# Masking the exponentials on GpSimd and VectorE instead of preloading transposed scores on TensorE, in an eight-stage attention chain

## The chip, the cores and the metric

The kernel runs on one core of a Trainium2 chip. The metric is device time in microseconds (us), the median of several runs. The trace is one further execution, recorded by the hardware profiler; its span runs from the first to the last instruction.

## The reference

The input is x, 16 sequences of 128 tokens by 256 features, in float32, with a context of the same shape. Four layers are applied one after another; together they are eight stages, named A0, A1, F0, A2, A3, A4, A5 and F1 in the kernel:

- A0: self-attention under a causal mask and a key mask. A1: attention over the context under the key mask. F0: feed-forward 256-1024-256 with Relu. Each is followed by adding the input and a layer norm with the unbiased standard deviation.
- A2: attention over the context, where mask[b, q, k] == 0 puts the score to -1e10. Norm.
- A3: attention over the context, scores multiplied by a weight per head and pair, and a mask per head and pair. Norm.
- A4: norm, attention over the context with no mask. A5: norm, self-attention under one mask of (query, key) that all sequences share. F1: norm, feed-forward with Gelu.

Every attention has 16 heads of 16 features: `softmax(mask(q k^T / 4)) v`, then an output product. A2 to A5 have biases on queries, keys, values and outputs. All arithmetic is float32.

## The kernel before

The 16 sequences are independent chains through the eight stages. Buffers exist for six of them at a time (SETS = 6), so that six are under way together. Each engine has one in-order list of steps, written out as strings of hexadecimal digits: a digit says which sequence does its next step on this engine (TENSOR, VECTOR, SCALAR, POOL, SYNC), and the steps of one sequence are those that `tensor_lane`, `vector_lane`, `scalar_lane`, `pool_lane` and `sync_lane` yield. PLACES gives each TensorE result one of eight PSUM banks. Semaphores alone tie the engines together.

One attention stage of one sequence goes so. TensorE transposes the input (xT, line 653), ScalarE copies it out (x_t, line 866), TensorE makes keys and queries with features on the partitions (K and Q, line 667). VectorE copies the keys twice, once multiplied by a 0/1 column for even heads and once for odd ones (k_eo, lines 986 and 990), and copies the queries, adding a bias (q_t, lines 999 and 1002). TensorE makes the scores with queries on the partitions (S, line 709), only to find each row's maximum: VectorE adds the mask and takes the maximum (L1018, one instruction and one read of its accumulator per head; L1023 where nothing is added). The maximum is split into two bf16 parts (high_low), transposed (mT) and copied (m_t, line 872). TensorE makes the scores again with keys on the partitions (ST, line 738), and adds minus the maximum to them by a small product (shift, line 749). In A0, A2 and A5 the four banks of ST are first filled with the mask, by one bf16 product of 128x512 each: `mask_bias(x, s)` against the identity (line 733). ScalarE takes the exponentials of four groups of four heads (exp, line 884, or 881 with a bias column in A1). TensorE multiplies by the values and a column of ones (PV, line 761), ScalarE copies the result (o_raw, line 889), TensorE transposes it (oT), VectorE divides (o_norm, lines 1044 and 1046), TensorE transposes again (nT), ScalarE copies (o_t, line 893), and TensorE makes the output product (O, line 660).

Then VectorE adds the residual (sum, line 1064), takes mean and variance (stats: `bn_stats` L1071, `bn_aggr` L1073, and a scale and epsilon L1075), GpSimd takes the root by a power (line 611), VectorE normalises (x_hat, line 1100), and GpSimd prepares the next residual (res, lines 621 to 629). In a feed-forward stage ScalarE makes the hidden units (h_t, line 903) in the buffers of exponentials, of which there are three.

Sync loads x, three masks and the context of each sequence (lines 513 to 523), the weights of each stage (line 530), and stores the result. In the first sequences the order is x of sequence 0, then x of sequence n with the three masks of sequence n - 1. The order lists begin with the transposes of five sequences on TensorE, and `bias` of all six on VectorE.

Of the kernel before, what the change touches and what calls it, by code (L numbers as in the profile page):

```python
# [17 lines left out]
KC = D // 128  # L18
# [3 lines left out]
EXP_BUFFERS, OUT_BUFFERS = 3, 2  # L22
# [34 lines left out]
PRELOADED = {"S": ("A1",), "ST": ("A0", "A2", "A5")}  # L57
CAPPED = [s for s in ("A0", "A2", "A5") if s not in PRELOADED["ST"]]
ADDED = [s for s in ("A0", "A2", "A5") if s not in PRELOADED["S"]]

# [17 lines left out]
POST_NORM = ("LN0", "LN1", "LN2", "LN3")  # L78

# [51 lines left out]
def vector_lane(x):  # L131
    yield "bias", "in"
    for s in STAGES:
        if x == 0:
            yield from (("folded", t) for t in FOLD_IN[s])
        if s in ATTN:
            if ATTN[s]["kv"] == "self":
                yield "k_eo", s
            yield "q_t", s
# [8 lines left out]
            if ATTN[s]["feeds"]:  # L148
                yield "k_eo", ATTN[s]["feeds"]
            if ATTN[s]["feeds"] and ATTN[ATTN[s]["feeds"]]["b"]:  # L150
                yield "v", ATTN[s]["feeds"]
            yield "o_norm", s
# [6 lines left out]
def scalar_lane(x):  # L159
    for s in STAGES:  # L160
        yield "x_t", s
        if s in FFN:
            yield from (("h_t", s, 0), ("h_t", s, 1))
            continue
        if ATTN[s]["kv"] == "self" and not ATTN[s]["b"]:
            yield "v", s
        yield "m_t", s
        yield from (("exp", s, j) for j in range(GROUPS))
        feeds = ATTN[s]["feeds"]
        yield "o_raw", s  # L170
        if feeds and not ATTN[feeds]["b"]:
            yield "v", feeds
        yield "o_t", s


def pool_lane(x):
    for s in STAGES:
        for n in LNS_AFTER[s]:
# [7 lines left out]
def sync_lane(x):  # L186
    yield from (("load_x", "in"), ("load_masks", "in"), ("load_ctx", "in"), ("load_weight", "in"), ("store", "out"))
# [4 lines left out]
21354113100100200244315050001000000110112020011310103012120222220100100020130022301233011121113133301100100012324040  # L192
21311042121020002000022221200130230021233040444411113111414103144121222230302002000200033333013001523454303022222204
22234123025300330000410231011004111155505540113441455443144455025050433334133332501004500001450441115411115155142551
20555015331135223112222225034031450504442061266146641144411431624662666662466415226124622332242631361633333432556623
13156625176666577366773422454457657657747757555744422656637752227672222333263333724743732356456747772776775375335727
24626742856768878873386666888733888838878485646333355768355548734684444554734586468885887478884834335877834439577776
99587997888999989999799789459864746956695855665644465459664875865498856499959898988945956754464594a798878aa77958a577
777a5a7a9aa9aaaa55556aa9a9a9576675a6859a9a96666867a67aaa5aa758575776aa5b7777bbabba7869996bbbb6bbbb6bb6ab9a99998b88a7
6969a9aabab76b66688688886a798a67a96987bbbbbb76bba6678686caacc7accaaaa8aabbcaccc8bacccc88cc887c7bca8877779ab8cbcbbb87  # L200
c7879b9b9978c999ccc7a88777d8dd8ccc9ccacaaac8998d88a8aaa88baac89dd9dddbdddcdddc9b9dcdbb9bbbbdbb8c8999bc9999b98ad9c88c
dc88e9eebabeedc9ccc9e9beeeeceececc9ceea9caeebbcbbcbbbba9ebe99ea999b9aa9cebaa9ceee9eeaaeecddaee9ab9addddddd9b9bdeccdc
aec9faffaefafadefdfffadccccdffffadffaefaaaabfedebbbdfbbbdfabecbeacbafdcbdddcffffddddfffeddafffdadfeefeedbaafdbfbfbba
deeeeeecffcebbbefbbcfbbebefdbdddbddddddffdbffdeffffcbbffbdfbdfdeeeefdedfdeeeddfddededdcececcccdcddfffddecfffffeffcef
ddfdcedddedecdeefeedfecfcedecffffffffeccefefdceefdffccccffecdceecfdffeeeeffceffcfecfcfcdfeffffeeeee
"""
VECTOR = """
01325411310100110000102234455001220202000012300003013121330111110102300012221100110021440422322424000001110220012330
03100212110132413333130104001010010000002220222002233200010530050434354325002200410151121211211111313340444410000501
13433133150124143105050005043241242222252221111505551252244415111500533011233311111514522534444406226624266664623134  # L210
33323363222246243343313166164236666636434444445452424353244645331735577565777223576746656722522223337533777266647437
77727323565424574346676536575455653555555557747286888888833333388774444848678653876688688548737547474768338484557585
85444394468995676699997946666666966888977559798559569888889996965794855664546469659577777777776777595558854a5aa79988
aaaa7a897a666a66aa9a5979755a797aaa9a7a6589799a97777788888888868685b868bbabbbb7ba6b6b6666a6a9ab6b89b9aab7a7bbb7b8b869
9a97aa6968a78a6ab88877777876cccacccc8caab888b8caaacbbccb9ca98999c99999999b7bccbc7878c78cb9caa88aaaaaaaa7daadda88888c
# [976 lines left out]
```

## Time and profile before

| | |
|---|---|
| Median of 3 runs | 1177.99 us (1177.74 to 1178.14) |
| The profiled execution's own time | 1174.8 us |
| Its span | 1173.0 us |
| TensorE matmuls busy | 1135.5 us, 97% |
| TensorE weight loads busy | 934.6 us, 80% |
| VectorE busy | 853.0 us, 73% |
| ScalarE busy | 475.9 us, 41% |
| GpSimd busy | 206.3 us, 18% |
| Mean granted TensorE clock | 0.994 of full speed |

Busy time is the time in which at least one instruction of the engine runs; instructions on one engine overlap a little, so the mean of one times its count can be more. Of the time outside TensorE's matmuls, 37.5 us, most lies in the first 30 us.

### The profile page before, as it was taken

The numbers are of one execution on the slowest core, as the hardware profiler recorded it, in microseconds if no ns is written. First come the engines' busy times: TensorE is split into PE (matmuls) and PEld (weight loads), VectorE is DVE, ScalarE is ACT, GpSimd is POOL, SyncE is SP. The second block draws the span as 40 slices with busy tenths as digits, with TensorE's granted clock in tenths as the row PEclk, the third lists the DMA queues.
The fourth block names the chain that finished last, engine by engine and source line by source line (L and its number), as shares of the span: only waits on it lengthen the run. The fifth ranks groups of instructions, "written<-read, shape, count | busy, mean of one in ns | idle before, by whom it ended". The sixth has DMA issues, their size and how long they took to land.

```text
span 1173.0 us, 36188 instructions
## 1 busy us (share of the span) xinstructions
PE 1135.5 (97%) x14100; PEld 934.6 (80%) x14100; DVE 853.0 (73%) x3467; ACT 475.9 (41%) x1118; POOL 206.3 (18%) x319
## 2 busy tenths in 40 slices
PE   4999999999999999999999999999999999999998
PEld 3878788878888888787887888887878887887678
DVE  4667679596789586777878767787697848687861
ACT  1243343334443434334444434434435344444353
POOL 0012212121111030212102021211111212211110
PEclk9999999899999999999999999999999999999999
DMA  6700010101010100101010010011001100011000
GB/s 245 321 2 2 2 47 2 46 2 47 18 58 11 42 14 6 47 19 47 14 52 13 6 47 18 2 63 47 14 6 52 58 3 2 6 51 47 2 3 18
DMA packets 22950, 44.05 MB, mean 38 GB/s; under 512 B 6528, under 2 KB 16896, under 8 KB 19712
## 3 DMA queue, kind: packets, MB, share of 16 engines
q1 hardware_dynamic: 21824, 40.30, 9.8%
q8 instruction: 116, 1.90, 0.7%
q10 hardware_dynamic: 960, 1.44, 0.3%
q14 instruction: 50, 0.41, 0.1%
HBM read 39.63 MB, written 2.10 MB: 36 GB/s over the span
## 4 chain that ended last, share of the span: by engine, by line
PE 82%; DVE 12%; issue 3%; SPq 1%; DMA 1%; ACT 0%; POOL 0%; DVEq 0%; POOLq 0%; ACTq 0%
PE bank L667 22%; PE bank L660 21%; PE bank L761 8%; PE bank L738 7%; PE bank L709 7%; PE bank L653 7%; PE bank L733 4%; DVE bank L1018 3%; PE bank L723 2%; PE bank L749 2%; DVE neg_max L1018 2%; DVE neg_max L1023 1%; PE bank L774 1%; PE bank L813 1%; DVE x_sum L1064 1%
## 5 line engine op out<-in xcount | busy, mean ns | idle before, releaser
L884 ACT ACTIVATE exps_t<-bank 128x512 f32<-128x512 f32 x320 | 169.4, 608 | 92.2 <-PE bank L749 91.9
L611 POOL TENSOR_TENSOR root<-var_eps,halves 128x1 f32<-128x1 f32 x128 | 74.0, 578 | 729.6 <-DVE var_eps L1075 729.2
L1018 DVE CUSTOM_DVE_ANT_0 bank<-bank,bias 128x128 f32<-128x128 f32 x512 | 130.0, 324 | 14.5 <-PE bank L709 14.1
L667 PE MATMUL bank<-x_t,weights_A 128*128 128x128 f32 x1024 | 134.9, 280 | 1.1 <-ACT x_t L866 1.0
L667 PEld LDWEIGHTS bank<-x_t,weights_A 128*128 128x128 f32 x1024 | 124.9, 193 | 9.1 <-issue 2.1
L667 PE MATMUL bank<-x_t,weights_F 128*128 128x128 f32 x1024 | 124.4, 277 | 0.8 <-ACT x_t L866 0.6
L667 PEld LDWEIGHTS bank<-x_t,weights_F 128*128 128x128 f32 x1024 | 118.8, 192 | 3.9 <-ACT x_t L866 1.3
L660 PE MATMUL bank<-weights_F,exps_t 128*128 128x256 f32 x512 | 120.4, 381 | 0.2 <-DVE x_t L1046 0.2
L709 PE MATMUL bank<-k_eo,q_t 32*128 32x256 f32 x1536 | 109.3, 398 | 3.0 <-DVE q_t L1002 2.2
L761 PE MATMUL bank<-exps_t,v_one 128*32 128x128 f32 x3072 | 108.5, 279 | 2.8 <-ACT exps_t L884 2.3
L903 ACT ACTIVATE exps_t<-bank,weights_F 128x128 f32<-128x128 f32 x256 | 73.0, 368 | 84.1 <-PE bank L667 83.7
L1018 DVE DVE_READ_ACCUMULATOR2_ANT neg_max<- 128x1 f32 x768 | 106.3, 138 | 0.0
L660 PEld LDWEIGHTS bank<-weights_F,exps_t 128*128 128x128 f32 x512 | 93.7, 190 | 12.5 <-DVE x_t L1046 0.4
L660 PE MATMUL bank<-weights_A,q_t 128*128 128x256 f32 x384 | 101.2, 389 | 2.2 <-ACT q_t L893 2.0
L738 PEld LDWEIGHTS bank<-q_t,k_eo 32*128 32x128 f32 x2560 | 80.4, 187 | 26.7 <-issue 25.3
L866 ACT COPY x_t<-bank 128x256 f32<-128x256 f32 x128 | 47.7, 378 | 132.6 <-PE bank L653 131.8
L761 PEld LDWEIGHTS bank<-exps_t,v_one 128*32 128x32 f32 x3072 | 77.7, 110 | 26.8 <-ACT exps_t L884 11.5
L889 ACT COPY o_raw<-bank 128x512 f32<-128x512 f32 x96 | 55.1, 587 | 107.7 <-PE bank L761 105.2
L738 PE MATMUL bank<-q_t,k_eo 32*128 32x128 f32 x2560 | 95.7, 284 | 0.6 <-issue 0.6
L1023 DVE TENSOR_REDUCE neg_max<-bank 128x4 f32<-128x512 f32 x128 | 81.1, 681 | 17.2 <-PE bank L709 17.0
L709 PEld LDWEIGHTS bank<-k_eo,q_t 32*128 32x128 f32 x1536 | 72.0, 185 | 19.9 <-issue 12.3
L986 DVE SCALAR_TENSOR_TENSOR k_eo<-bank,parity,k_bias_A 128x256 f32<-128x256 f32 x128 | 55.9, 478 | 35.2 <-PE bank L667 21.9
(103 smaller groups left out, 1820.0 us busy)
## 6 DMA issues: line engine op xcount, KB each, us to landing
weight<-in_fside SPq DMA_DIRECT2D x16, 1024.0 KB, 4.9
weights_A<-in_weights_A SPq DMA_DIRECT2D x4, 1028.0 KB, 18.1
weights_F<-in_weights_F SPq DMA_DIRECT2D x2, 2054.0 KB, 16.4
drop_raw<-in_drop SPq DMA_DIRECT2D x16, 256.0 KB, 5.3
x_hat<-in_x SPq DMA_DIRECT2D x16, 128.0 KB, 3.1
out<-x_sum SPq DMA_DIRECT2D x16, 128.0 KB, 1.7
ctx_t<-in_ctx_t SPq DMA_DIRECT2D x13, 128.0 KB, 3.7
rows_A<-in_rows_A SPq DMA_DIRECT2D x3, 512.0 KB, 19.8
```

Of the source, the lines that this page charges most:

```text
L611: nc.gpsimd.tensor_tensor(root[x][:], var_eps[x][:], halves[:, e:e + 1], ALU.pow).then_inc(done["root"], 1)
L653: mm = nc.tensor.matmul(dst[:, 128 * c:128 * c + 128], src[:, 128 * c:128 * c + 128], id32[:], start=True, stop=True, is_transpose=True)
L660: mm = nc.tensor.matmul(dst, left[:, c, :], right[:, c, :], start=(c == 0), stop=(c == total - 1))
L667: mm = nc.tensor.matmul(dst[:, 128 * f:128 * f + 128], w[:, c, 128 * f:128 * f + 128], tokens_t[:, c, :], start=(c == 0), stop=(c == KC - 1))
L709: mm = nc.tensor.matmul(score_bank(x, "S", s, j)[:, 256 * c:256 * c + 256], q_t[x][group_rows(j), c, :], k_eo[x][group_rows(j), c, :, :], ...
L738: mm = nc.tensor.matmul(score_bank(x, "ST", s, j)[:, 128 * n:128 * n + 128], k_eo[x][group_rows(j), n // 2, n % 2, :], q_t[x][group_rows(j ...
L761: mm = nc.tensor.matmul(bank((x, "PV", s, 0))[32 * n:32 * n + 32, 128 * j:128 * j + 128], v_one[x][:, VE * head(j, n):VE * head(j, n) + 2 ...
L884: nc.scalar.activation(dst, score_bank(x, "ST", s, j)[:], ACT.Exp, scale=DH ** -0.5).then_inc(done["exp"], 1)
L903: ins = nc.scalar.activation(hidden(x, s)[:, f, :], src[:, 128 * n:128 * n + 128], ACT.Gelu if FFN[s]["gelu"] else ACT.Relu, bias=b_1[s][: ...
L986: ins = nc.vector.scalar_tensor_tensor(out=k_eo[x][:, :, odd, :], in0=src, scalar=parity[:, odd:odd + 1], in1=k_bias[s][:, odd, :].unsquee ...
L1018: ins = nc.vector.tensor_tensor_reduce(out=heads[:, n, :], in0=heads[:, n, :], in1=mask_bias(x, s), scale=-1.0, scalar=2.0 ** 126, op0=ALU ...
L1023: nc.vector.tensor_reduce(neg_max[x][:, j, :], heads, AX_X, ALU.max, negate=True).then_inc(done["max"], 1)
```

## The change

- The mask products of line 733 are gone from A0, A2 and A5. The exponentials are taken unmasked and then lowered. In A0 ScalarE adds the key mask as a bias column, and GpSimd sets the pairs of a later key to zero with `affine_select`. In A2 and A5 VectorE takes the minimum with a bf16 tile of 2^-100 or 2 (0 or 2 in A5), made from transposed masks. TensorE's PV waits for that step instead of for exp.
- ScalarE takes over the query copy with its bias (two Identity instructions where there is one) and the even and odd key copies of A0 and A1, which have no bias.
- The variance: the residual sum also accumulates its row sum, a small instruction makes minus the mean, and ScalarE squares the centred row with an accumulator, into x_hat as scratch. `bn_stats` and `bn_aggr` remain for LN5 alone.
- Key masks of all sequences are loaded by two DMAs behind x of sequence 0. The pair mask comes in two versions (plain and transposed), in three buffers, the first three behind the weights of F0. The A0 weights come in two halves.
- All order strings and bank places are new. TensorE has the same 1607 steps; its order now starts with the transposes of sequences 1 to 5 and then K, Q of 1. It ends with one sequence alone: behind the last Y of sequence e stand PV, oT, nT, O, xT, H and Y of f. Before, the last 33 us held steps of c, d, e and f.

```diff
-PRELOADED = {"S": ("A1",), "ST": ("A0", "A2", "A5")}
+LEAST = 2.0 ** -100
+PRELOADED = {"S": ("A1",), "ST": ()}
...
+SQUARED = [n for n in LN if n != "LN5"]
+SUMMED = [s for s in STAGES if LNS_AFTER[s]]
...
+        def load_keys(queue):
+            queue.dma_start(key_rows[:].rearrange("p b n -> p (b n)"), dram["kmask"].rearrange("b c d e -> (c d) (b e)")
+                            .broadcast_to([128, B * N])).then_inc(keys_loaded, 16)
+            queue.dma_start(key_cols[:], dram["kmask_t"]).then_inc(keys_loaded, 16)
+        def load_pairs(queue, x):
+            at = x % PAIR_BUFFERS
+            queue.dma_start(ik_raw[at][:], whole("ik", x)).then_inc(pairs_loaded[at], 16)
+            queue.dma_start(ik_t_raw[at][:], whole("ik_t", x)).then_inc(pairs_loaded[at], 16)
...
                 load_x(sp, 0)
+                load_keys(sp)
                 for x in range(1, SETS):
                     load_x(sp, x)
-                    load_masks(sp, x - 1)
-                load_masks(sp, SETS - 1)
...
+                def hide_later(x, s, j):
+                    pool.wait_ge(done["exp"], nth(x, "exp", s, j))
+                    e = exps_t[EXP_AT[x, s]][:, slots(j), :]
+                    nc.gpsimd.affine_select(out=e, in_=e, compare_op=ALU.is_ge, fill=0.0, base=0,
+                                            pattern=[[0, GH], [1, N]], channel_multiplier=-1).then_inc(done["later"], 1)
...
-                    if masked:
-                        if s == "A5":
-                            pe.wait_ge(sxs_made, 1)
-                        else:
-                            pe.wait_ge(done["bias"], nth(x, "bias", "in"))
-                        for j in range(GROUPS):
-                            nc.tensor.matmul(free_bank((x, "ST", s), j)[:], mask_bias(x, s), four(idb[:]), start=True, stop=True)
...
-                    pe.wait_ge(done["exp"], nth(x, "exp", s, j))
+                    made = "later" if s == "A0" else "keep" if s in ("A2", "A5") else "exp"
+                    pe.wait_ge(done[made], nth(x, made, s, j))
...
+                    elif kind == "k_eo":
+                        src = free_keys(act, x, s)
+                        act.wait_ge(parity_made, 4)
+                        for odd in range(2):
+                            ins = nc.scalar.activation(k_eo[x][:, :, odd, :], src, ACT.Identity, scale=parity[:, odd:odd + 1])
...
+                            for c in range(KC):
+                                ins = nc.scalar.activation(q_t[x][:, c, :], src[:, c, :], ACT.Identity,
+                                                           bias=q_bias[s][:, c:c + 1])
...
+                    elif kind == "square":
+                        act.wait_ge(means_made, norm_turn(VECTOR_ORDER, "sum", x, LN[s]["after"][1], SUMMED))
+                        nc.scalar.activation(x_hat[x][:], x_sum[x][:], ACT.Square, bias=neg_mean[x][:, 0:1],
+                                             accum_out=squares[x][:]).then_inc(done["square"], 1)
...
+                    nc.vector.tensor_scalar(pair_most[x][:], ik_t_raw[at][:], 0.0, 2.0, ALU.not_equal, ALU.mult
+                                            ).then_inc(pairs_kept, 1)
+                    dve.wait_ge(pairs_kept, 2 * nth(x, "pairs", "in"))
+                    nc.vector.tensor_scalar(pair_most[x][:], pair_most[x][:], LEAST, None, ALU.max).then_inc(done["pairs"], 1)
...
+                def keep_seen(x, s, j):
+                    dve.wait_ge(done["exp"], nth(x, "exp", s, j))
...
+                    nc.vector.tensor_tensor(e, e, four(most), ALU.min).then_inc(done["keep"], 1)
...
+                    if s in SUMMED:
+                        nc.vector.tensor_tensor_reduce(out=x_sum[x][:], in0=src[:, 0:D], in1=residual[:], scale=1.0, scalar=0.0,
+                                                       op0=ALU.add, op1=ALU.add, accum_out=row_sum[x][:]).then_inc(done["sum"], 1)
+                        dve.wait_ge(done["sum"], nth(x, "sum", s))
+                        nc.vector.tensor_scalar(neg_mean[x][:], row_sum[x][:], -1.0 / D, None, ALU.mult).then_inc(means_made, 1)
...
+                    if n in SQUARED:
+                        dve.wait_ge(done["square"], nth(x, "square", n))
+                        nc.vector.tensor_scalar(var_eps[x][:], squares[x][:], 1.0 / (D - d["ddof"]),
+                                                0.0 if d["on_root"] else d["eps"], ALU.mult, ALU.add).then_inc(done["stats"], 1)
+                        return
```

## Rows read from the trace of the kernel before

**Rows 1.** The page's first part: busy time and share of the span by engine.
```profile
PE 1135.5 (97%) x14100; PEld 934.6 (80%) x14100; DVE 853.0 (73%) x3467; ACT 475.9 (41%) x1118; POOL 206.3 (18%) x319
```
**Rows 2.** Chain that ended last, by engine.
```profile
PE 82%; DVE 12%; issue 3%; SPq 1%; DMA 1%; ACT 0%; POOL 0%; DVEq 0%; POOLq 0%; ACTq 0%
```
**Rows 3.** Busy time by stretch; columns: length, PE, PEld, DVE, ACT, POOL, clock, DMA.
```profile
0.00:10.00 10.00, 0.00 (x0) 0.00 (x0) 1.82 (x23) 1.28 (x1) 1.54 (x12) 1.00 0.61 193
10.00:20.00 10.00, 6.29 (x30) 5.12 (x31) 2.51 (x16) 1.86 (x5) 0.00 (x0) 1.00 0.47 148
20.00:30.00 10.00, 7.82 (x78) 6.74 (x77) 8.74 (x48) 0.75 (x2) 0.00 (x0) 1.00 1.03 409
...
1140.00:1173.00 33.00, 29.74 (x262) 26.25 (x250) 6.17 (x18) 12.91 (x36) 2.55 (x4) 1.00 0.05 17
```
**Rows 4.** Line 733 among the groups by line on PE.
```profile
L733 PE MATMUL bank<-idb,bias 128*128 128x512 bf16 x128 | 34.6, 388 | 1.3 <-DVE v_one L1121 0.4 <-DVE k_eo L990 0.4 <-DVE neg_max L1018 0.2
...
L733 PE MATMUL bank<-idb,sxs_bias 128*128 128x512 bf16 x64 | 16.7, 380 | 0.0
```
**Rows 5.** Pieces of the chain that ended last: start, length, what.
```profile
1138.08 0.86 PE bank L733 x4
```
**Rows 6.** The start in order of time: start, length, engine, line.
```profile
10.73 1.09 PE L653 MATMUL bank<-id,x_hat 128*128 128x128 f32 x4 [10.73 <-DMA x_hat<-in_x]
...
16.60 4.08 PE L667 MATMUL bank<-x_t,weights_A 128*128 128x128 f32 x24 [0.46 <-ACT x_t L866]
...
22.87 1.15 PE L709 MATMUL bank<-k_eo,q_t 32*128 32x256 f32 x16 [2.18 <-DVE q_t L1002]
```
**Rows 7.** Groups by line on DVE.
```profile
L1018 DVE DVE_READ_ACCUMULATOR2_ANT neg_max<- 128x1 f32 x768 | 106.3, 138 | 0.0
L1071 DVE BATCH_NORM_STATS2 bn<-x_sum 128x6 f32<-128x256 f32 x128 | 54.0, 422 | 2.0
L1133 DVE SCALAR_TENSOR_TENSOR weight<-drop_raw,weight 128x512 f32<-128x512 uint8 x64 | 44.6, 697 | 0.9
...
L1064 DVE TENSOR_TENSOR x_sum<-bank,x_hat 128x256 f32<-128x256 f32 x80 | 33.5, 420 | 58.7 <-PE bank L660 58.4
L999 DVE TENSOR_TENSOR q_t<-bank,q_bias_A 128x256 f32<-128x256 f32 x80 | 33.4, 419 | 28.9 <-PE bank L667 28.7
L990 DVE TENSOR_SCALAR k_eo<-bank,parity 128x256 f32<-128x256 f32 x64 | 27.9, 477 | 21.5 <-PE bank L667 11.8 <-issue 9.7
...
L1073 DVE BATCH_NORM_AGGREGATE mean_var<-bn 128x2 f32<-128x6 f32 x128 | 23.3, 182 | 4.4
...
L1075 DVE TENSOR_SCALAR var_eps<-mean_var 128x1 f32<-128x1 f32 x128 | 19.7, 154 | 4.4
```
**Rows 8.** Groups by line on ACT.
```profile
L884 ACT ACTIVATE exps_t<-bank 128x512 f32<-128x512 f32 x320 | 169.4, 608 | 92.2 <-PE bank L749 91.9
L903 ACT ACTIVATE exps_t<-bank,weights_F 128x128 f32<-128x128 f32 x256 | 73.0, 368 | 84.1 <-PE bank L667 83.7
...
L866 ACT COPY x_t<-bank 128x256 f32<-128x256 f32 x128 | 47.7, 378 | 132.6 <-PE bank L653 131.8
L881 ACT ACTIVATE exps_t<-bank,col_bias 128x512 f32<-128x512 f32 x64 | 39.3, 688 | 22.0 <-PE bank L749 21.8
...
L903 ACT ACT_TABLE_LOAD x15 | 19.2, 1283 | 0.3
```
**Rows 9.** Groups by line on POOL.
```profile
L611 POOL TENSOR_TENSOR root<-var_eps,halves 128x1 f32<-128x1 f32 x128 | 74.0, 578 | 729.6 <-DVE var_eps L1075 729.2 <-PE bank L653 0.2
L621 POOL TENSOR_TENSOR x_hat<-x_hat,rows_A 128x256 f32<-128x256 f32 x48 | 35.0, 730 | 103.0 <-PE bank L653 102.0 <-DVE x_hat L1100 0.9
...
L590 POOL TENSOR_SCALAR_AFFINE_SELECT id<-id 128x128 f32<-128x128 f32 x1 | 0.3, 292 | 0.2 <-POOL causal L585 0.2
```
**Rows 10.** DVE and POOL instructions in order of time, around 754 us.
```profile
754.06 1.08 DVE L1133 SCALAR_TENSOR_TENSOR weight<-drop_raw,weight 128x512 f32<-128x512 uint8 x1
...
754.68 1.05 POOL L626 TENSOR_TENSOR x_hat<-x_hat,rows_F 128x256 f32<-128x256 f32 x1
```

More of the change, by code:

```diff
@@ L54 @@
 STAGES = ["A0", "A1", "F0", "A2", "A3", "A4", "A5", "F1"]
[L57 to L59 removed]
+LEAST = 2.0 ** -100
+PRELOADED = {"S": ("A1",), "ST": ()}
+ADDED = ("A0", "A2", "A5")
 LN = {
@@ L147, in vector_lane @@
             yield "high_low", s
-            if ATTN[s]["feeds"]:
+            if ATTN[s]["feeds"] and ATTN[ATTN[s]["feeds"]]["b"]:
                 yield "k_eo", ATTN[s]["feeds"]
+            if s in ("A2", "A5"):
+                yield from (("keep", s, j) for j in range(GROUPS))
             if ATTN[s]["feeds"] and ATTN[ATTN[s]["feeds"]]["b"]:
@@ L163, in scalar_lane @@
             yield from (("h_t", s, 0), ("h_t", s, 1))
+            yield from (("square", n) for n in LNS_AFTER[s] if n in SQUARED)
             continue
+        if ATTN[s]["kv"] == "self" and not ATTN[s]["b"]:
+            yield "k_eo", s
+        yield "q_t", s
         if ATTN[s]["kv"] == "self" and not ATTN[s]["b"]:
@@ L169, in scalar_lane @@
         feeds = ATTN[s]["feeds"]
+        if feeds and not ATTN[feeds]["b"]:
+            yield "k_eo", feeds
         yield "o_raw", s
@@ L173, in scalar_lane @@
         yield "o_t", s
+        yield from (("square", n) for n in LNS_AFTER[s] if n in SQUARED)
 def pool_lane(x):
     for s in STAGES:
+        if s == "A0":
+            yield from (("later", s, j) for j in range(GROUPS))
         for n in LNS_AFTER[s]:
@@ L422, in program @@
         ctx_loaded = sems("ctx_loaded")
-        masks_loaded = sems("masks_loaded")
+        keys_loaded = sem("keys_loaded")
+        first_loaded = sem("first_loaded")
+        pairs_loaded = [sem(f"pairs_loaded{x}") for x in range(PAIR_BUFFERS)]
         stored = sems("stored")
@@ L426, in program @@
                                               "H", "Y", "fold")}
-        done |= {k: sem(f"done_{k}") for k in ("x_t", "v_copy", "m_t", "exp", "o_raw", "o_t", "h_t")}
-        done |= {k: sem(f"done_{k}") for k in ("bias", "folded", "k_eo", "q_t", "v", "times", "lower", "max", "high_low", "o_norm", "sum",
+        done |= {k: sem(f"done_{k}") for k in ("x_t", "square", "v_copy", "k_copy", "q_t", "m_t", "exp", "o_raw", "o_t", "h_t")}
+        done |= {k: sem(f"done_{k}") for k in ("bias", "pairs", "folded", "k_eo", "v", "times", "lower", "max", "high_low", "keep", "o_norm", "sum",
                                                "stats", "x_hat")}
-        done |= {k: sem(f"done_{k}") for k in ("root", "res")}
+        done |= {k: sem(f"done_{k}") for k in ("root", "res", "later")}
         key_bias_made = sem("key_bias_made")
+        pairs_kept = sem("pairs_kept")
         high_made = sem("high_made")
         recip_made = sem("recip_made")
+        rows_summed = sem("rows_summed")
+        means_made = sem("means_made")
         bn_made = sem("bn_made")
@@ L551, in _ @@
                 load_stage(sp, "F0")
+                for x in range(PAIR_BUFFERS):
+                    load_pairs(sp, x)
                 load_stage(sp, "A2")
@@ L780, in shift_products, with weights_loaded @@
                     return mm
+                def weights_loaded(s, part):
+                    if s == "A0" and part == "first":
+                        pe.wait_ge(first_loaded, 16)
+                    else:
+                        pe.wait_ge(stage_loaded[s], all_loaded(s))
                 def norm_folded(s, part):
```

281 lines of the change are left out of this document (158 added, 123 removed).

## The prediction, made before the changed kernel was run

> **What bounds the kernel now.** I read the busy shares first: TensorE 97%, VectorE 73%, ScalarE 41%, GpSimd 18% [rows 1]. A busy TensorE need not be the bound, so the chain of waits comes next: followed back from the end, 82% of the span is TensorE work, 12% VectorE's [rows 2]. Both views say that TensorE's instruction stream is the limit nearly everywhere, and that in some stretches VectorE is late for it. So work taken off TensorE shortens the span at full price, unless what remains is held up elsewhere; work taken off or put on the others counts only through waits.
>
> Then the stretches. The span of 1173.0 less 1135.5 busy leaves 37.5 us in which no matmul runs. I split it with the view by stretch [rows 3]: 10.0 + 3.7 + 2.2 = 15.9 us in the first 30 us; 3.3 us in the last 33 us; so 18.3 us in the 1110 us between, 1.6% of them. These three parts are predicted separately.
>
> **The mask products.** There are 128 + 64 = 192 of them [rows 4]. Their own duration, 0.38 us, is latency and overlaps the next; on the chain four of them take 0.86 us [rows 5], 0.215 us each. 192 x 0.215 = 41.3 us go. The scores behind them stay as they are. Since TensorE is on the path, 41.3 us is the first term; bounds are 36 us (if the 12% of the chain that is VectorE's gives its share back as waiting) and 51 us (the two groups' busy time, 34.6 + 16.7 [rows 4], which counts overlap).
>
> **The start.** TensorE begins at 10.73 us, held by x, and the first keys at 16.60, because the order wants five transposes first and the last x is issued late, behind twelve mask DMAs; then it waits 2.18 us for queries which VectorE copies behind its mask work, itself late by those DMAs [rows 6]. After the change two larger DMAs stand in place of those twelve ahead of the last x, and the first queries and keys go through ScalarE, which does nothing then. The first ten microseconds carry 193 GB/s [rows 3]: 0.77 MB of x, 0.26 MB of keys and the 1 MB of weights at that rate are 10.5 us. So I put the first keys at 11 us and no wait of 2 us behind them: idle 11 in place of 15.9, a gain of 5 us. Bounds: 0 if the weights now arrive last, 8 if the DMAs move as fast as between 20 and 30 us (409 GB/s [rows 3]). The pair masks and their transposed copies, 32 of 64 KB, leave the start; later Sync queues them in its list as it did the old ones, with nothing urgent behind, so nothing.
>
> **The end.** Before, four sequences fill TensorE to within 3.3 us, most of it the last sum and store. In the new order sequence f is alone behind e's last product. Its chain there: exponentials 0.6 each and minima 0.7 each, begun behind the sum of e, 2.4 us beyond what TensorE does meanwhile; o_raw 0.6, reciprocal and division 0.7, o_t 0.4; sum, mean, square, scale, root and x_hat 0.5 + 0.2 + 0.5 + 0.2 + 0.6 + 0.4 = 2.4; x_t 0.4; a dozen hand-overs of 0.1, 1.2 (durations as in [rows 7 to 9]). That is 8.1 us, plus the same 2.6 for last sum and store: 10.7 against 3.3, a loss of 7.5 us. Bounds: 4 (if half of those waits are covered by e's last matmuls) and 12 (if e and f, two sequences where there were four, already leave gaps a stage earlier).
>
> **VectorE.** Off it go the query copies, 96 x 0.419 = 40.2; the plain key copies, 27.9; 112 of 128 `bn_stats`, 47.3, and `bn_aggr`, 20.4: 135.8 us [rows 7]. On it come 128 minima over 128x512 with two SBUF inputs. The nearest row is L1133, 0.697 [rows 7]: 89.2 us. Below, they could cost 0.42, the row for half the elements (53.8 us); above, 1.08, what L1133 took once (138 us). Further 112 small mean instructions like L1075, 17.2; 112 sums with an accumulator, dearer by one read of 0.138, 15.5, and at least nothing; the pair masks' two more small ones for 16 sequences, about 7. Together 129 us. Net -7: VectorE stays near 846 us, 75% of the shorter span. It is no more the bound than before, but TensorE leaves it 41 us less room.
>
> That 1.08 has a cause in the trace: L1133 at 754.06 overlaps a GpSimd addition at 754.68, and both are longer than usual (1.08 for 0.697, 1.05 for about 0.73) [rows 7, 9, 10]. The Trainium skill, GPSIMD Engine Reference, section Specifications, says the same: the SBUF interfaces are shared, with contention for VectorE instructions with two SBUF inputs. The new minima are such instructions. With GpSimd busy a fifth of the time and 0.35 us more where they meet, 128 x 0.22 x 0.35 = 10 us on VectorE, which wipes out its net saving and is in my range, not in the sum.
>
> **ScalarE.** 160 biased halves of queries at 0.368 and 16 copies at 0.378 are 65; 64 key copies at 0.378 + 0.080 (what a column operand adds, 0.688 - 0.608) are 29; 112 squares at 0.46 + 0.14 are 67 [rows 8]. 476 + 161 = 637 us, 56%. Hidden by TensorE, for which ScalarE waited most of the time (idle before its rows, all ended by PE [rows 8]). If the cover is gone, each query copy is late by 0.2 us: 80 x 0.2 = 16 us at worst.
>
> **GpSimd.** 64 selects over 128x512. At 128x128 one took 0.292 [rows 9]. Bounds are 0.3 (all fixed cost) and 1.35 (0.73 for 256 elements with two inputs, scaled with the overhead kept); I take 0.9: 58 us, 206 becomes 264 us, 23%. Behind a select that waits for its exponential stand roots of other sequences; behind those x_hat on VectorE. Five other sequences cover it.
>
> **Latency per sequence.** A0 gains 4 x 0.9, A2 and A5 4 x 0.7 less their overlap with exponentials, norms 0.3 more. Some 10 us on a chain which has six sequences' time, 1173 x 6 / 16 = 440 us, for itself. Nothing in the middle; its 18.3 us I leave at 18.3.
>
> **The sum.** 1173.0 - 41.3 - 5.0 + 7.5 = 1134.2 us of span. The profiled execution took 1.8 us more than its span: 1136.0. The median of runs is 3.2 us above the profiled one (1177.99 against 1174.8), so runs should give 1139 us.
>
> **Rivals.**
> 1. The gain is held back. VectorE and ScalarE become late in more stretches: with 41 us less TensorE work, a stretch in which VectorE ends last gains nothing. For it speaks the chain's 12%; against it, only 1.6% of the middle is idle. Price: 12% of 41 us, the 10 us of contention, and a few us of queries on ScalarE: 18 us, 1157 us.
> 2. The start gives 8 and the end takes only 2, since f's lone chain is partly covered, and the middle's idle time shrinks by 5, as its waits for m_parts, exponentials and queries are of 0.5 us each and in new places: 1178 - 41.3 - 8 + 2 - 5 = 1126 us.
> 3. Slower: table loads. A load takes 1.283 us [rows 8]. Today they come only where Gelu and Exp alternate in ScalarE's list (29 times, 31 in the new one); Copy and Relu need none. If Square isn't in Exp's table, each of 112 squares brings two loads, 2.57 us, 287 us on ScalarE: 924 us, above VectorE, and 2.6 us more in each norm, with exponentials queued behind. It outweighs the gain of 39 us once 0.35 us of each 2.57 surfaces on TensorE; at a sixth it does, 1186 us. The Trainium skill, ScalarE: Activation LUTs, section Table sets, says that cheap functions such as relu, copy and identity are in every set, and doesn't list square there. This trace agrees for relu and copy, and shows nothing of the other two.
> 4. The change doesn't do what it says: if the exponentials' extra hand-over delayed PV so that TensorE idles 0.4 us at each of 96 PV groups of A0, A2 and A5, the product's saving would be gone: 1178 us. Against it: PV of other sequences stand between in the order.
>
> **How the numbers follow.** The forecast 0.57, rival 1 0.19, rival 2 0.20, rival 3 0.02, rival 4 0.02. A change is told from none here at about 0.2%, 2.4 us. Faster: 0.57 + 0.19 + 0.20 = 0.96, to which half of rival 4 adds 0.01; same 0.01; slower 0.02. The likeliest case alone reaches from 1130 to 1148, by the bounds of the start, the end and the mask products. The range of eight in ten goes to rivals 1 and 2: 1125 to 1156 us.
>
> **What would show it.** TensorE busy near 1094 us and no line 733; first keys on TensorE near 11 us; the last 35 us with 10 us idle; VectorE's share at 75%, ScalarE's at 56%, minima near 0.7 us, selects near 0.9; table loads about 30 as now. The prediction is wrong if TensorE's idle time in the middle passes 30 us (rival 1), if table loads pass 200 (rival 3), or if matmuls left in place change their pitch.

## The result, and the profile after

The changed kernel takes 1159.94 us (median of 3 runs, 1159.59 to 1161.37); before it was 1177.99. The ratio is 0.9881 (95% interval 0.9853 to 0.9910): faster by 18 us, where 39 were forecast, and outside the range of 1125 to 1156. The profiled execution took 1159.94 us, its span is 1157.7. Two single executions, of 1415 us in experiment 5 and of 3640 us in experiment 10, stood far apart from the others of their kernels and are in none of the ratios below.

First the busy time by engine, from the page of the changed kernel; it answers to [rows 1].
```profile
PE 1106.9 (96%) x13908; PEld 921.1 (80%) x13908; DVE 841.3 (73%) x3468; ACT 618.6 (53%) x1584; POOL 258.8 (22%) x383
```
The 192 products are gone (14100 less 13908 matmuls). VectorE, ScalarE and GpSimd are where the prediction put them (846, 637 and 264). TensorE isn't: 1106.9 us busy where 1135.5 - 41.3 = 1094.2 were expected, and 1157.7 - 1106.9 = 50.8 us idle, where 18.3 + 11 + 10.7 = 40 were. So more than half of what is missing lies in TensorE's busy time, which is not all work at full pace.

Where that idle time lies is told by the view by stretch (columns as in [rows 3]), of the changed kernel:
```profile
0.00:30.00 30.00, 19.79 (x163) 16.79 (x164) 13.78 (x112) 9.39 (x23) 1.55 (x12) 1.00 0.95 343
30.00:100.00 70.00, 68.66 (x912) 56.59 (x910) 42.53 (x199) 36.70 (x94) 21.25 (x33) 0.98 0.25 100
100.00:1000.00 900.00, 881.40 (x11298) 738.27 (x11297) 686.53 (x2780) 498.83 (x1284) 212.66 (x304) 1.00 0.08 27
1000.00:1124.70 124.70, 114.08 (x1368) 91.18 (x1367) 89.92 (x341) 62.26 (x158) 22.07 (x33) 0.99 0.07 25
1124.70:1157.70 33.00, 22.98 (x177) 18.24 (x175) 8.54 (x41) 11.40 (x28) 1.27 (x2) 0.79 0.02 8
```
and of the kernel before, the two stretches that the rows ahead of the prediction don't have:
```profile
100.00:1000.00 900.00, 888.80 (x11184) 733.91 (x11183) 683.12 (x2752) 376.68 (x885) 171.45 (x258) 1.00 0.08 26
1000.00:1140.00 140.00, 134.19 (x1710) 106.52 (x1712) 108.02 (x419) 57.56 (x132) 23.51 (x34) 1.00 0.06 23
```
Length less the first busy number is TensorE's idle time. In the first 30 us it is 10.2 (15.9 before, 11 predicted). In the last 33 us it is 10.0 (3.3 before, 10.7 predicted). Between them it is 30.6 us (1.34 + 18.60 + 10.62), where it was 18.4 (1.36 + 11.20 + 5.81) and was left at 18.3. The last stretch has one number more: the granted clock is 0.79, where it was 1.00 before [rows 3].

The view of TensorE's waits, changed kernel (for what, us in total, times, longest):
```profile
PE bank L707 <- DMA x_hat<-in_x: 9.3, 1, 9.3
PE bank L707 <- DVE x_hat L1205: 6.9, 10, 2.7
PE bank L808 <- DVE exps_t L1083: 6.1, 18, 1.1
PE bank L721 <- ACT x_t L931: 3.8, 8, 0.6
```
and one row of the same view of the kernel before:
```profile
PE bank L653 <- DVE x_hat L1100: 1.4, 3, 0.5
```
The third row is a wait that the kernel before didn't have: L808 is PV, and L1083 the minimum in place. The second is the norm, 6.9 us for 1.4. What the new instructions cost, by the groups by line:
```profile
L1083 DVE TENSOR_TENSOR exps_t<-exps_t,pair_most 128x512 f32<-128x512 f32 x64 | 44.9, 750 | 0.0
L1083 DVE TENSOR_TENSOR exps_t<-exps_t,sxs_most 128x512 f32<-128x512 f32 x64 | 44.4, 739 | 9.8 <-ACT exps_t L971 9.7
...
L1158 DVE DVE_READ_ACCUMULATOR2_ANT row_sum<- 128x1 f32 x112 | 9.2, 82 | 0.0
L953 ACT ACTIVATE x_hat<-x_sum,neg_mean 128x256 f32<-128x256 f32 x112 | 57.2, 511 | 85.1 <-DVE neg_mean L1161 84.5
L953 ACT ACTIVATION_READ_ACCUMULATOR x_hat<-x_sum,neg_mean 128x1 f32 x112 | 21.3, 190 | 0.0
L990 ACT ACT_TABLE_LOAD x16 | 20.5, 1283 | 0.3
L971 ACT ACT_TABLE_LOAD x14 | 18.0, 1283 | 5.2 <-PE bank L714 5.0
...
L645 POOL TENSOR_SCALAR_AFFINE_SELECT exps_t<-exps_t 128x512 f32<-128x512 f32 x64 | 43.5, 709 | 100.6 <-ACT exps_t L968 100.5
```
Minima at 0.74 to 0.75 us, 89.3 us in all (0.697 and 89.2 predicted); selects 0.71 (0.9). Squares bring no table loads: there are 30 in these two groups and 32 in all.

The start, TensorE in order of time (start, length); it answers to [rows 6]: transposes at 9.33 us, keys at 12.73 where it was 16.60, and no wait for the queries ahead of L763.
```profile
9.33 2.94 PE L707 MATMUL bank<-id,x_hat 128*128 128x128 f32 x10 [9.33 <-DMA x_hat<-in_x]
12.73 5.17 PE L721 MATMUL bank<-x_t,weights_A 128*128 128x128 f32 x24 [0.46 <-ACT x_t L931]
17.83 1.15 PE L763 MATMUL bank<-k_eo,q_t 32*128 32x256 f32 x16
```

The end. First the last sequence alone, in order of time, then the same stretch cut into windows (the number behind POOL's is the granted clock):
```profile
1133.08 0.43 PE L808 MATMUL bank<-exps_t,v_one 128*32 128x128 f32 x8 [1.12 <-DVE exps_t L1083]
...
1138.90 2.05 PE L714 MATMUL bank<-weights_A,q_t 128*128 128x256 f32 x4 [0.55 <-ACT q_t L980]
1143.65 0.66 PE L707 MATMUL bank<-id,x_hat 128*128 128x128 f32 x2 [2.71 <-DVE x_hat L1205]
1144.86 6.57 PE L721 MATMUL bank<-x_t,weights_F 128*128 128x128 f32 x32 [0.55 <-ACT x_t L931]
1151.27 3.62 PE L714 MATMUL bank<-weights_F,exps_t 128*128 128x256 f32 x16
```
```profile
1124.70:1133.00 8.30, 7.26 (x85) 6.15 (x83) 4.45 (x31) 5.90 (x14) 0.00 (x0) 1.00 0.01 2
1133.00:1138.00 5.00, 2.65 (x38) 1.34 (x38) 2.50 (x6) 0.59 (x1) 0.00 (x0) 0.90 0.08 26
1138.00:1144.00 6.00, 2.74 (x8) 1.47 (x6) 1.16 (x5) 0.97 (x3) 0.97 (x2) 0.50 0.00 0
1144.00:1151.00 7.00, 6.45 (x32) 6.17 (x31) 0.00 (x0) 2.80 (x6) 0.30 (x1) 0.53 0.00 0
```
TensorE is busy half of the five microseconds from 1133 on, and the granted clock falls from 1.00 (2.4 GHz) through 0.90 to 0.50 (1.2 GHz). At that level the output projection takes 2.05 us, and the 32 matmuls of the last feed-forward's first half 6.57. In the kernel before, with TensorE full there, they took:
```profile
1154.20 1.03 PE L660 MATMUL bank<-weights_A,q_t 128*128 128x256 f32 x4
...
1163.03 3.81 PE L667 MATMUL bank<-x_t,weights_F 128*128 128x128 f32 x32 [0.55 <-ACT x_t L866]
```
1.0 + 2.8 us, with two pairs of short transposes (0.66 for the 0.41 that they take in experiment 4) 4.3 us. The last 33 us aren't all of it. A few us earlier, behind a wait of 1.12 us, 16 matmuls take 3.51 us, which in experiment 4 take 2.02; the stretch from 1110 to 1124.7 has a granted clock of 0.88. So the rows show 4.3 + 1.5 = 5.8 us.
```profile
1116.81 3.51 PE L721 MATMUL bank<-x_t,weights_A 128*128 128x128 f32 x16 [0.55 <-ACT x_t L931]
```
The Trainium skill, TensorE: Matmul & The Clock Gate, section Why this matters for your kernels, warns of idle gaps between bursts of matmuls, behind which the clock is back at half. The trace agrees that the clock falls where TensorE waits between bursts, but the page speaks of single gaps longer than any in this stretch: in the last stretch the clock is down after idle pieces of 1.12, 0.85 and 0.90 us, before the one wait of 2.71.

A wait in pieces also lengthens the busy time. The 32 matmuls of one PV step take 1.08 us in one piece, as in experiment 2 at this place. In the last sequence here each eight of them wait for their minimum and take 0.43 us, 1.72 together, besides the waits between.

### The profile page after: what moved, and what is told of

Same layout as the page of the kernel before. It is cut to its first block and busy times, and to the rows that moved or that the text cites. A ratio compares the mean times of both kernels' runs of the same rounds, so it can differ in the third digit from the quotient of the medians.

```text
span 1157.7 us, 36414 instructions
## 1 busy us (share of the span) xinstructions
PE 1106.9 (96%) x13908; PEld 921.1 (80%) x13908; DVE 841.3 (73%) x3468; ACT 618.6 (53%) x1584; POOL 258.8 (22%) x383
## 5 line engine op out<-in xcount | busy, mean ns | idle before, releaser
L663 POOL TENSOR_TENSOR root<-var_eps,halves 128x1 f32<-128x1 f32 x128 | 76.9, 602 | 609.9 <-DVE var_eps L1171 588.1
L971 ACT ACTIVATE exps_t<-bank 128x512 f32<-128x512 f32 x256 | 135.7, 605 | 34.3 <-PE bank L795 33.8
L721 PE MATMUL bank<-x_t,weights_A 128*128 128x128 f32 x1024 | 139.3, 284 | 2.7 <-ACT x_t L931 2.1
L721 PEld LDWEIGHTS bank<-x_t,weights_A 128*128 128x128 f32 x1024 | 127.3, 197 | 12.1 <-ACT x_t L931 4.5
L721 PE MATMUL bank<-x_t,weights_F 128*128 128x128 f32 x1024 | 127.9, 281 | 2.8 <-ACT x_t L931 1.7
L721 PEld LDWEIGHTS bank<-x_t,weights_F 128*128 128x128 f32 x1024 | 121.6, 195 | 9.1 <-ACT x_t L931 3.1
L808 PE MATMUL bank<-exps_t,v_one 128*32 128x128 f32 x3072 | 114.5, 277 | 8.2 <-DVE exps_t L1083 6.1
L763 PE MATMUL bank<-k_eo,q_t 32*128 32x256 f32 x1536 | 107.7, 396 | 2.6 <-issue 1.7
L808 PEld LDWEIGHTS bank<-exps_t,v_one 128*32 128x32 f32 x3072 | 74.5, 109 | 40.1 <-DVE exps_t L1083 15.1
L953 ACT ACTIVATE x_hat<-x_sum,neg_mean 128x256 f32<-128x256 f32 x112 | 57.2, 511 | 85.1 <-DVE neg_mean L1161 84.5
L784 PEld LDWEIGHTS bank<-q_t,k_eo 32*128 32x128 f32 x2560 | 82.1, 186 | 16.8 <-issue 12.7
L968 ACT ACTIVATE exps_t<-bank,col_bias 128x512 f32<-128x512 f32 x128 | 80.4, 695 | 27.9 <-PE bank L795 27.8
L1116 DVE TENSOR_REDUCE neg_max<-bank 128x4 f32<-128x512 f32 x128 | 81.4, 681 | 18.4 <-PE bank L763 18.4
L763 PEld LDWEIGHTS bank<-k_eo,q_t 32*128 32x128 f32 x1536 | 72.6, 185 | 20.0 <-issue 13.6
```

What stands on the lines that cost most here:

```text
L663: nc.gpsimd.tensor_tensor(root[x][:], var_eps[x][:], halves[:, e:e + 1], ALU.pow).then_inc(done["root"], 1)
L721: mm = nc.tensor.matmul(dst[:, 128 * f:128 * f + 128], w[:, c, 128 * f:128 * f + 128], tokens_t[:, c, :], start=(c == 0), stop=(c == KC - 1))
L763: mm = nc.tensor.matmul(score_bank(x, "S", s, j)[:, 256 * c:256 * c + 256], q_t[x][group_rows(j), c, :], k_eo[x][group_rows(j), c, :, :], ...
L784: mm = nc.tensor.matmul(score_bank(x, "ST", s, j)[:, 128 * n:128 * n + 128], k_eo[x][group_rows(j), n // 2, n % 2, :], q_t[x][group_rows(j ...
L808: mm = nc.tensor.matmul(bank((x, "PV", s, 0))[32 * n:32 * n + 32, 128 * j:128 * j + 128], v_one[x][:, VE * head(j, n):VE * head(j, n) + 2 ...
L953: nc.scalar.activation(x_hat[x][:], x_sum[x][:], ACT.Square, bias=neg_mean[x][:, 0:1], accum_out=squares[x][:]).then_inc(done["square"], 1)
```

## The experiments

Each was run beside the kernel before on its chip; ratios are to that kernel. A difference of 0.001 is 1.2 us. The intervals are 0.2 to 0.3% either way, so a difference between two of these ratios is uncertain by 3 to 5 us. The changed kernel's 0.9881 was taken apart from the ratios below, beside a kernel before at 1177.99 us where theirs is at 1173 to 1174; differences against it carry that too.

**1. The products alone taken away**, in the old orders. The masks of the transposed scores are left out; nothing stands for them.
```
-                        for j in range(GROUPS):
-                            nc.tensor.matmul(free_bank((x, "ST", s), j)[:], mask_bias(x, s), four(idb[:]), start=True, stop=True)
```


> The kernel before, with its own orders, and with the 192 mask products taken out and nothing put in their place (the exponentials of A0, A2 and A5 are left unmasked). Theory (the products were worth their full price, and the changed kernel gives part of it back in waits for the steps that it adds): 1178 - 41 = 1137 us, within 4. Rival (the products hid something, weight loads or late engines, so that their removal is worth half): 1150 to 1158 us whatever the orders.

0.9786 (0.9760 to 0.9811): 25.6 us below its kernel before (1148.57 against 1174.16). Page:
```profile
PE 1102.5 (96%) x13908; PEld 926.4 (81%) x13908; DVE 852.4 (74%) x3467; ACT 477.3 (42%) x1118; POOL 206.3 (18%) x319
```
TensorE's busy time falls by 33.0 us of the 41.3, and its idle time rises from 37.5 to 43.1. The products are not worth their full price; some 16 us are missing. Only 5.6 of them are idle time. The 8.3 that busy time falls short by stand mostly in the scores behind the products, which the prediction took to stay as they are (busy time, mean ns; first the kernel before, then this one):
```profile
L738 PE MATMUL bank<-q_t,k_eo 32*128 32x128 f32 x2560 | 95.7, 284 | 0.6 <-issue 0.6
L731 PE MATMUL bank<-q_t,k_eo 32*128 32x128 f32 x2560 | 104.6, 286 | 1.4 <-DVE k_eo L983 0.6 <-DVE v_one L1114 0.3
```
The group is busy 8.9 us longer without the products in front. What holds it up was not taken apart.

**2. The lowering taken away** from the changed kernel: no selects, no minima, PV waits for the exponential.
```
-                    made = "later" if s == "A0" else "keep" if s in ("A2", "A5") else "exp"
+                    made = "exp"
```


> The changed kernel with its 64 selects on GpSimd and 128 minima on VectorE left out, so that PV follows the exponentials at once (the exponentials are left partly unmasked). Theory (PV's waits for the lowering steps, and VectorE's 89 us in them, are the largest part of what came back): 10 to 16 us less than 1160, about 1147 us. Rival (the new orders are loose by themselves): under 4 us less, 1156 to 1160 us.

0.9755 (0.9737 to 0.9773), 0.0126 below the changed kernel: the lowering costs 15 us. The prediction had it in the lone chain at the end only, and at no time in the middle. Page, and two rows of the end:
```profile
PE 1098.9 (96%) x13908; PEld 921.0 (81%) x13908; DVE 755.5 (66%) x3340; ACT 617.6 (54%) x1584; POOL 208.8 (18%) x319
```
```profile
1121.26 1.08 PE L808 MATMUL bank<-exps_t,v_one 128*32 128x128 f32 x32
...
1130.45 5.35 PE L721 MATMUL bank<-x_t,weights_F 128*128 128x128 f32 x32 [0.55 <-ACT x_t L931]
```
Half of the 15.6 us of span are idle time (43.2 for 50.8) and half TensorE's busy time (8.0 us). Of the latter, 4.2 are PV's (its group is busy 110.3 us for 114.5), and 2.7 are the clock's, which falls later at the end of this kernel: the output projection takes 1.10 us for 2.05, the transposes 0.41 for 0.66 twice, the last feed-forward's first half 5.35 for 6.57.

**3. The variance back on VectorE**, in the new orders: `bn_stats`, `bn_aggr` and a plain sum; squares skipped.
```
-SQUARED = [n for n in LN if n != "LN5"]
+SQUARED = []
```


> The changed kernel with the variance as before: bn_stats and bn_aggr on VectorE for all eight norms, a plain residual sum, no squares on ScalarE. Orders unchanged. Theory (the norm's way over ScalarE and back is late for the next transpose): TensorE's waits for x_hat fall from 6.9 us towards the 1.4 of before, about 1155 us. Rival (VectorE is what is short, and bn_stats costs it 35 us net): 1160 to 1168 us.

1.0109 (1.0082 to 1.0137): 27 us slower than the changed kernel, and far outside what either side expected. Page and waits:
```profile
PE 1121.5 (94%) x13908; PEld 928.2 (78%) x13908; DVE 886.6 (75%) x3468; ACT 561.6 (47%) x1360; POOL 258.8 (22%) x383
```
```profile
PE bank L708 <- DVE x_hat L1207: 15.2, 23, 2.5
```
45 us more on an engine that is 73% busy cost 27 us. Its busy share says little; the waits for the norm double (15.2 for 6.9 us). Half of the 29.3 us of span is TensorE's busy time again (14.6), at a mean granted clock of 0.984 for 0.990.

**4. Dummy products near the end** of the changed kernel: 40 of 128x512 with constant operands (the text below says 39; the numbers of the edit add up to 40, and 13948 matmuls ran for 13908), in two banks that nothing reads by then, placed among the last 35 steps of TensorE's order. They add no result.
```
+                filler = {-35: 1, -30: 1, -26: 2, -25: 4, -24: 2, -21: 2, -12: 5, -8: 3, -7: 4, -6: 2, -5: 12, -4: 2}
+                    for _ in range(filler.get(at, 0)):
+                        nc.tensor.matmul(banks[3 if at < -20 else 6][:], idb[:], pick[:]..., start=True, stop=True)
```


> The changed kernel with 39 products of 128x512 added between TensorE's last 36 steps, into a bank that nobody reads, where it waited. They compute nothing that is used. Theory (in the last 45 us the granted clock falls to half since TensorE idles, which costs about 5 us): the granted clock stays at full, O of f takes 1.0 us and not 2.05, H 3.8 and not 6.6: 1155 us. Rival (the clock isn't what makes the end long, or the added products delay the steps behind them): 1160 us or more.

0.9835 (0.9817 to 0.9853), 1154.25 us: 5.4 us below the changed kernel, and the fastest version of all that compute everything. Its end in order of time:
```profile
1116.97 2.02 PE L721 MATMUL bank<-x_t,weights_A 128*128 128x128 f32 x16
...
1137.33 1.10 PE L714 MATMUL bank<-weights_A,q_t 128*128 128x256 f32 x4
1138.27 2.75 PE L844 MATMUL bank<-pick,idb 128*128 128x512 bf16 x12
...
1142.10 3.81 PE L721 MATMUL bank<-x_t,weights_F 128*128 128x128 f32 x32
```
Work that does nothing (L844) fills the wait of 2.7 us, the 16 matmuls are at 2.02 and the 32 back at 3.81, and the window of the last 33 us shows the granted clock at 1.00:
```profile
1119.00:1152.20 33.20, 29.19 (x241) 20.73 (x239) 9.93 (x49) 13.56 (x32) 1.27 (x2) 1.00 0.03 9
```
The 5.8 us by the rows and the 5.4 by this run agree within its interval.

**5 and 6. A lighter VectorE.** The kernel before without `bn_stats` and `bn_aggr` (a constant variance, 77 us less work), and the same with the products gone too.
```
-                    nc.vector.bn_stats(bn[x][:], x_sum[x][:]).then_inc(bn_made, 1)
-                    nc.vector.bn_aggr(mean_var[x][:], bn[x][:]).then_inc(aggr_made, 1)
```


> The kernel before with bn_stats and bn_aggr left out of all 128 norms (the variance is a constant, so the layer norms are not computed): 77 us less work on VectorE, products kept. Theory A (VectorE is late in stretches and TensorE is the bound in the rest): a few us, 4 to 10, about 1167 us in this chip's terms (before 1174). Theory B (the order on TensorE with its drains alone sets the time): under 3 us.

> The kernel before with both left out: the 192 mask products (masks not applied to the exponentials) and bn_stats and bn_aggr. Without the products it took 25.6 us less and not 41. Theory A (what is missing went into waits for VectorE): most of it comes back: 1174 - 41 - 5 = 1128 us, so that the products are worth 38 us and more on a light VectorE. Theory B (removing the products exposes something of TensorE's own, weight loads or drains): they are worth 26 again: before_light less 26, about 1145 us.

0.9937 (0.9919 to 0.9955) and 0.9680 (0.9656 to 0.9704). In the old orders 77 us less on VectorE (72.5 of its busy time) give 7.3 us. With it the products are worth (0.9937 - 0.9680) x 1173 = 30.1 us, where without it they were worth 25.6. So VectorE's load explains some 5 of the 16 us that are missing, and even these are no more than the intervals leave open; the other 11 it doesn't.

**7 and 8. The lowering taken apart.** In the first the minima are computed as before (0.75 us each) but into a scratch tile, and in A2 and A5 PV waits for the exponential alone: their load stays, their place in the chain goes. In the second they are left out. In both the selects stay, and PV of A0 waits for them.
```
-                    nc.vector.tensor_tensor(e, e, four(most), ALU.min)
+                    nc.vector.tensor_tensor(aside[...][:], e, four(most), ALU.min)
```


> The changed kernel where the 128 minima are computed for the same time into a scratch tile, and PV waits for the exponentials alone (the minima have no effect on the result). It has VectorE's load without the hand-over. Theory A (the loss is the latency between exp and PV): close to the run without minima, within 3 us. Theory B (the loss is the 89 us that VectorE spends): close to the changed kernel, 1160 in that kernel's terms on this chip, and 8 us or more above the run without minima.

> The changed kernel without the 128 minima (A2 and A5 unmasked in the exponentials), selects on GpSimd kept. Without both it was 15 us faster. If VectorE carries the loss: 11 to 14 us of the 15 here, about 1147. If GpSimd's selects and their place before PV carry it: under 6 us, 1154 or more.

0.9838 (0.9812 to 0.9865) and 0.9778 (0.9757 to 0.9799). Against the 0.9881 of the changed kernel and the 0.9755 without any lowering, the hand-over costs 5 us, the minima's load on VectorE 7, and the selects 3. Only the 7 is clear of the intervals. The 5 is at their edge, but has rows behind it, the 6.1 us of waits above; the 3 isn't told from nothing. With minima aside the row of waits for them is gone, and PV waits for exponentials 2.4 us (1.5 in the changed kernel):
```profile
PE bank L809 <- ACT exps_t L974: 2.4, 4, 0.7
```

**9. The products added to the changed kernel**, beside its selects and minima, so that the masks act twice.
```
+                        for j in range(GROUPS):
+                            nc.tensor.matmul(free_bank((x, "ST", s), j)[:], mask_bias(x, s), four(idb[:]), start=True, stop=True)
```


> The changed kernel with the 192 mask products added to it again ahead of the transposed scores of A0, A2 and A5; its selects and minima stay, so the masks act twice. It measures what the products are worth in the new orders. Full price (the prediction's term): 192 x 0.215 = 41.3 us above the changed kernel, ratio to the kernel before about 1.02. Rival, that in any fixed order a part of TensorE's stream is cover for other engines' chains: as much as their removal gave in the old orders, 25.6 us (30.2 on a light VectorE), ratio about 1.007. TensorE's idle time tells them apart: it stays near 51 us by the first, and falls to 35 or so by the second.

1.0163 (1.0141 to 1.0186): 33 us above the changed kernel. Page:
```profile
PE 1146.4 (96%) x14100; PEld 934.3 (78%) x14100; DVE 841.2 (71%) x3468; ACT 619.0 (52%) x1584; POOL 257.5 (22%) x383
```
39.5 us more busy, 5 us less idle (45.8 for 50.8). Neither side is met: 33 of 41 lies between the full price and the 25.6 of the old orders. By these two differences, the price of an instruction on the bound engine depends on the order around it.

**10. The query copies on VectorE**, in the new orders, each where ScalarE did it by the trace.
```
-        yield "q_t", s        # in ScalarE's lane
+            yield "q_t", s    # in VectorE's lane
```


> The changed kernel with all 96 query copies on VectorE as before, each put into VectorE's order where ScalarE did it by the trace. VectorE gets 96 x 0.42 = 40 us more (841 to 881 us), ScalarE loses about 65. Theory, VectorE is the short engine whatever its share says: as the variance on VectorE cost 27 us for 45 us of work, this costs 20 to 27 us, ratio to the kernel before about 1.005. Rival, that only work in the norms' chain costs: the copies have a score's time to themselves, ScalarE's relief gives something back, and it costs 0 to 8 us, ratio about 0.99.

1.0022 (1.0006 to 1.0039): 16.5 us slower, for 34 us more on VectorE (875.0 busy) and 50 less on ScalarE. Between the two, nearer to the theory.

**11 and 12. A better end.** To the kernel with the dummy products, the mask by products again in the last sequence's A5, ahead of both kinds of scores, in place of masked maxima and minima; and the same in three stages (A5 of the last two sequences, A2 of the last).
```
+LAST = [(15, "A5")]
-                    masked = s in PRELOADED["S"]
+                    masked = s in PRELOADED["S"] or (x, s) in LAST
```


> The changed kernel with the 39 dummy products near the end, and besides in the last sequence's A5 alone the mask is added by products (four ahead of its scores, four ahead of its transposed scores) in place of VectorE's masked maxima (16 of 0.249 become 4 reductions of 0.6: 1.6 us less) and of its four minima (0.683 each behind exponentials of 0.57: about 1 us less). The sequence is alone on the chip then, so both count in full: 2 to 2.6 us below the kernel with the dummy products alone, ratio to the kernel before about 0.981. Rival, the eight products of 0.215 and covered waits take it back: no difference, 0.9835.

> The same in three stages near the end: A5 of the last two sequences and A2 of the last. Theory, in the last 60 us VectorE's work is dearer than TensorE's: each further stage gives 0.5 to 1.5 us, 3 to 5 us below the kernel with the dummy products alone, ratio about 0.980. Rival, TensorE is still full at those two stages: 1.7 us more in each, 1 to 3 us worse than with the last sequence's alone.

0.9840 (0.9819 to 0.9861) and 0.9862 (0.9841 to 0.9883), against 0.9835 with the dummy products alone. The theory falls in both. The chain of waits of the first shows why:
```profile
1123.73 1.06 PE bank L715 x4
1124.79 3.57 PE bank L722 x32
1128.36 1.73 PE bank L715 x8
1130.09 0.06 PE bank L881
1130.15 0.86 PE bank L789 x4
```
Between the last scores and the last transposed scores TensorE makes the last sequence's own values (L715 x4, 1.06 us) and still does the feed-forward of the sequence ahead (L722 x32 and L715 x8, 5.3 us). The maxima ran under it, and shortening them by 1.6 us gives nothing, while the four products (L789, 0.86) are on the path. The last sequence isn't alone yet at that point; I had taken it to be.

## Why the prediction was wrong

Point by point, by its own steps.

- **What bounds the kernel.** TensorE's stream, held up here and there. Right in kind. But of "work taken off or put on the others counts only through waits" the waits were then priced as if 1.6% of idle time meant that there were none to come.
- **The mask products, 41.3 us.** Too high. 25.6 in the old orders (experiment 1), 33 in the new (9). Even the lower bound of 36, drawn from VectorE's 12% of the chain, is above both. "The scores behind them stay as they are" fails in the old orders, where they are busy 8.9 us longer. VectorE's load accounts for about 5 of the 16 us missing there (5, 6), if for any.
- **The start, -5.0.** Right: idle 10.2 for 15.9, keys at 12.73 (11 predicted).
- **The end, +7.5.** The idle time is right, 10.0 against 3.3. The step lacks a term: a stretch with that much idle time in short pieces loses the clock, and the work that remains takes longer. 4.3 us by the rows of the last 33 us, 5.8 with the stretch ahead of them, 5.4 by experiment 4.
- **VectorE, net -7, "no more the bound than before".** The sum is right (841 against 846), the conclusion wrong, and this is the step that failed: **the minima were set off against work taken away, and the middle's idle time was left at 18.3; it is 30.6.** Two things are wrong in it. The minima stand in the chain from exponential to PV, which the query and key copies and `bn_stats` that they were set off against did not: 5 us (the changed kernel less experiment 7), with 6.1 us of waits in the rows. And their load delays what is queued behind them on VectorE: 7 us (experiment 7 less 8). The lowering as a whole costs 15 us, of which only the lone chain's part at the end was in a term.
- **GpSimd and ScalarE.** Busy times right within 5 and 18 us. Contention is visible, as at 611 us, where two minima took 1.89 us beside two selects with 1.67:
```profile
610.76 1.67 POOL L645 TENSOR_SCALAR_AFFINE_SELECT exps_t<-exps_t 128x512 f32<-128x512 f32 x2
611.08 1.89 DVE L1083 TENSOR_TENSOR exps_t<-exps_t,sxs_most 128x512 f32<-128x512 f32 x2
```
  but on the mean it is small. The 91 minima beside which nothing runs on GpSimd take 0.683 us on the mean, the 37 others 0.895, so 37 x 0.21 = 8 us of VectorE's time in all; the prediction's range held 10. What of these 8 us reaches the span was not run.
- **Rivals.** The first (the gain held back, 1157 us, chance 0.19) is what happened: the middle's idle time passed the 30 us that the prediction named as its mark. Of its reasons, a VectorE late in more stretches is borne out (7 and 8, 10); that its 1157 lies so near 1160 is partly luck, as it doesn't hold the clock at the end. The third (table loads) is refuted by 32 loads. The fourth's mechanism is real, 18 waits of PV for minima with 6.1 us in all, a sixth of the 38 us that it was priced at. Its count was wrong as well: A0, A2 and A5 of 16 sequences are 48 steps of PV in four groups each, 192 and not 96.

The balance: 1139 forecast, 1160 measured, 21 us. In the span it is 23.5 (1157.7 for 1134.2; the forecast then added 1.8 + 3.2 us from span to median, where 2.2 came). By the rows the 23.5 are 12.3 us of idle time in the middle and 12.7 of busy time, 5.8 of it the clock's, less 1.5 at the two ends. By the experiments the lowering costs 15 us and the clock at the end 5.4, but the two overlap: 2.7 us of the lowering's price are the clock's, so that together they are some 18. No run leaves out both. Even so far as they close the gap, it doesn't mean that the rest was right: the products gave 8 to 16 us less than their price, and what made up for it is work moved off VectorE, priced at nothing in the prediction, that is worth 27 us (variance) and 16.5 us (queries) in the new orders. These are the costs of undoing each part in orders made for the change; what each would have given in the old ones was not run (but 5, where 77 us less on VectorE gave 7.3), and they don't add up to one sum. Open stay, too, the 11 us of experiment 1 that VectorE's load doesn't explain. A fixed order in which each product was also cover for some other engine's chain would do it, and both the rise from 25.6 to 33 us in other orders and the scores that take longer without the products speak for that, but no run separates it.

## What to carry to other kernels

An engine's busy share isn't its slack: here 73% busy, VectorE gave or took 0.1 to 0.6 us for each microsecond of work moved, so work added to it in the chain of a stage needs its own term, even if as much is taken off elsewhere. Work removed from the bound engine of a kernel whose orders are fixed returned 60 to 80% of its time; put the rest into the sum, not only into the range. Look for the price in the busy time of the bound engine too: waits in short pieces and a lower clock stand there and not in its idle time. And where one sequence ends alone, count the clock as well as the gaps; a few matmuls that compute nothing can pay for themselves.

## What the runs showed of the hardware

- The granted clock fell to 0.50 after a stretch in which TensorE was busy half of the time, with no single gap over 1.2 us before the fall began (0.90 in the window 1133 to 1138), and 7 us of nearly full work at 0.53 followed. It had fallen once before, to 0.88 on the mean from 1110 to 1124.7. 40 products of no use, of which at most 12 stand together, kept it at 1.00.
- Eight PV matmuls on their own take 0.43 us, 32 in one piece 1.08.
- A 128x512 minimum with two SBUF inputs takes 0.683 us with GpSimd idle and 0.895 on the mean beside GpSimd's work.
- Square and Identity ran on ScalarE between exponentials without a table load: 112 squares and 224 uses of Identity with 32 loads in all. A square of 128x256 with accumulator takes 511 ns, and the read behind it 190.
- A select of 128x512 on GpSimd takes 709 ns on the mean, 2.4 times the 292 of 128x128 [rows 9] for four times the elements.
- The accumulator read behind a sum of 256 elements takes 82 ns, not the 138 of the one behind the maxima [rows 7].
